# Sixteen batches of a fused convolution, attention and expert block: loops written out, value tiles spread, the residual added by identity products, the next input loaded by channel halves

## What is computed

```python
# 1. convolution attention over channels (32 inner channels)
q, k, v = conv1x1(x, Wq, bq), conv1x1(x, Wk, bk), conv1x1(x, Wv, bv)
x = conv1x1(softmax(q @ k) @ v, Wo, bo) * gamma + x
# 2. differential attention over the tokens, 8 heads of width 32
t = tokens(x); n = layer_norm(t)
a = softmax(q1 @ k1.T / s) - lam * softmax(q2 @ k2.T / s)       # q1, k1, q2, k2, v from n
t = t + group_norm(a @ v) @ out_w.T + out_b
# 3. shared expert and 8 routed experts (the best 2 are kept), hidden width 128
n = layer_norm(t)
t = t + shared(n) + sum_e(combine[e] * expert_e(n))
```

## Time and profile before

| what | us |
|---|---|
| median of 3 runs | 6143.56 |
| lowest and highest run | 6142.13, 6154.33 |
| the profiled execution's own time | 6151.38 |
| span of its trace | 6149.6 |
| TensorE busy | 5867.3 (95% of the span) |
| VectorE busy | 4669.8 (76%) |
| ScalarE busy | 3217.5 (52%) |
| GpSimd busy | 3090.5 (50%) |
| mean granted clock of TensorE | 0.977 of full |

### The profile page before, as it was taken

How to read it: one execution, slowest core, us unless ns; L and a number is a source line. 1 busy time by engine, 2 the same in 40 slices (tenths; PEclk the granted TensorE clock), 3 DMA queues, 4 the chain that set the end, 5 groups by cost and what they waited for, 6 DMA issues and landing times.

```text
span 6149.6 us, 126831 instructions
## 1 busy us (share of the span) xinstructions
PE 5867.3 (95%) x41264; PEld 3809.3 (62%) x41264; DVE 4669.8 (76%) x6583; ACT 3217.5 (52%) x5788; POOL 3090.5 (50%) x1382
## 2 busy tenths in 40 slices
PE   6999999999999999999999999999999999999999
PEld 3566566655656556566665766657666566665666
DVE  5867778687786877868778787786877778677786
ACT  3645546455564545636456464554645546455464
POOL 2826638175380744807447083571825728256281
PEclk8999999999999999999999999999999999999999
DMA  2212222222222212222222221222212222121221
GB/s 75 58 46 61 58 53 54 60 51 58 51 50 60 55 56 52 48 60 57 56 51 48 62 58 54 53 50 60 59 48 55 49 61 59 46 58 47 65 58 46
DMA packets 148332, 338.95 MB, mean 55 GB/s; under 512 B 38224, under 2 KB 60880, under 8 KB 139216
## 3 DMA queue, kind: packets, MB, share of 16 engines
q1 hardware_dynamic: 146128, 329.32, 22.0%
q10 hardware_dynamic: 1536, 1.05, 0.1%
HBM read 90.49 MB, written 17.30 MB: 18 GB/s over the span
## 4 chain that ended last, share of the span: by engine, by line
PE 76%; DVE 9%; issue 7%; ACT 3%; DMA 2%; POOL 2%; DVEq 0%; ACTq 0%; SPq 0%; POOLq 0%
PE psum L1049 17%; PE psum L1265 16%; PE psum L1190 14%; PE psum L1211 13%; PE psum L1349 6%; DVE minus_max L773 6%; PE psum L1218 4%; PE psum L1309 2%; POOL prob_sums L379 2%; PE psum L1196 1%; PE psum L1098 1%; DMA prob_sums<-combine_rows_dram 1%; ACT probs L523 1%; DVE small L688 1%; PE psum L1111 0%
## 5 line engine op out<-in xcount | busy, mean ns | idle before, releaser
L379 POOL TENSOR_TENSOR prob_sums<-probs 128x1024 f32<-128x1024 f32 x752 | 1795.7, 2389 | 2892.2 <-ACT probs L523 2559.2
L523 ACT ACTIVATE probs<-psum 128x512 f32<-128x512 f32 x4096 | 2214.2, 595 | 1376.0 <-PE psum L1265 1341.1
L773 DVE TENSOR_REDUCE minus_max<-psum 128x1 f32<-128x1024 f32 x2048 | 2400.3, 1209 | 413.6 <-PE psum L1190 409.6
L1265 PE MATMUL psum<-stack 98*128 98x512 f32 x4096 | 1430.7, 434 | 2.5 <-DVE max_rows L783 1.8
L379 POOL TENSOR_TENSOR prob_sums<-prob_sums,probs 128x1024 f32<-128x1024 f32 x512 | 1219.3, 2381 | 44.4 <-ACT probs L523 6.6
L1190 PE MATMUL psum<-stack 96*128 96x512 f32 x4096 | 1198.8, 406 | 25.2 <-DVE minus_max L773 24.5
L1211 PE MATMUL psum<-probs,v_tokens 128*32 128x256 f32 x16384 | 1126.2, 389 | 5.8 <-ACT probs L523 5.8
L1265 PEld LDWEIGHTS psum<-stack 98*128 98x128 f32 x4096 | 702.5, 191 | 543.4 <-ACT probs L523 326.5
L1190 PEld LDWEIGHTS psum<-stack 96*128 96x128 f32 x4096 | 757.1, 192 | 258.8 <-DVE minus_max L773 68.0
L1211 PEld LDWEIGHTS psum<-probs,v_tokens 128*32 128x32 f32 x16384 | 423.4, 109 | 487.4 <-issue 271.0
L1049 PE MATMUL psum<-act_hi,w_hi 128*128 128x512 f32 x1730 | 690.5, 399 | 19.4 <-DVE act_lo L752 11.0
(11 more groups left out here) (153 smaller groups left out, 4680.3 us busy)
## 6 DMA issues: line engine op xcount, KB each, us to landing
stack<-stage SPq DMA_DIRECT2D x1024, 128.0 KB, 3.0
stack<-stage SPq DMA_DIRECT2D x256, 256.0 KB, 3.0
prob_sums<-combine_rows_dram SPq DMA_DIRECT2D x128, 256.0 KB, 3.8
stage<-combine_rows_dram SPq DMA_DIRECT2D x128, 256.0 KB, 4.3
x_tile<-x_dram SPq DMA_DIRECT2D x17, 1024.0 KB, 4.9
x_tile<-o_head SPq DMA_DIRECT2D x480, 32.0 KB, 1.9
stack<-max_rows SPq DMA_DIRECT2D x512, 4.0 KB
y_dram<-residual SPq DMA_DIRECT2D x16, 512.0 KB, 2.8
```

The source lines that it names most:

```text
L379: nc.gpsimd.tensor_tensor(total, first, probs[:, k % NP, :], ALU.add).then_inc(sum_pool, 1)
L523: nc.scalar.activation(probs[:, k % NP, half * HALF:(half + 1) * HALF], ps[:, exp_bank(k) + half, :], ACT.Exp).then_inc(p_ready, 1)
L773: v.tensor_reduce(nm[:, u % 2, q:q + 1], flat_in, AX.X, ALU.max, negate=True).then_inc(ring_free, 1)
L1265: mm(ps[:, exp_bank(k) + half, :], stack[0:KS, s, 1, kt * P:(kt + 1) * P], stack[0:KS, s, 0, half * HALF:(half + 1) * HALF], start=True, s ...
```

## The change

All loops over batches become straight code, on all five engines, so each wait compares with a constant. The value tiles stand behind the scores 0 to 3 and 5 to 7 of unit 0, and tile 7 behind the second score of unit 1. The residual goes into PSUM banks 0 to 3 by four plain float32 products with the identity, ahead of the output projection, which then accumulates onto it; what is left for the other engines is to add the bias and move the sum out, for channel tile 0 on ScalarE and for channel tile 1 on VectorE. `norm_groups(b, 1)` stands after the first high half of `project_out` and no longer after both. The next input is loaded by two transfers, one for each channel tile; the first waits only for `on_hi` of tile 0. `conv_vk` goes by channel tiles, with a wait for each.

```diff
-VALUES_BEHIND = {("score", 0, q): (q,) for q in range(6)}
-VALUES_BEHIND["turn", 0] = (6, 7)
+VALUES_BEHIND = {("score", 0, q): (tt,) for q, tt in ((0, 0), (1, 1), (2, 2), (3, 3), (5, 4), (6, 5), (7, 6))}
+VALUES_BEHIND["score", 1, 1] = (7,)
...
-                sp.wait_ge(on_lo, b * NH * CT + NH * CT)
-                sp.dma_start(xin[:, :, :], x[following].rearrange("(t p) n -> p t n", p=P)).then_inc(x_in, 16)
+                for t in range(CT):
+
+                    if t == 0:
+                        sp.wait_ge(on_hi, b * NH * CT + NH)
+                    else:
+                        sp.wait_ge(on_lo, b * NH * CT + NH * CT)
+                    sp.dma_start(xin[:, t, :], x[following].rearrange("(t p) n -> p t n", p=P)[:, t, :]).then_inc(x_in[t], 16)
...
-            with sp.Fori(0, B - 1) as b:
-                batch(b, b + 1)
-
-            batch(B - 1, B - 1)
+            for b in range(B):
+                batch(b, min(b + 1, B - 1))
...
-            with act.Fori(0, B) as b:
+            for b in range(B):
...
+                for half in range(NH):
+                    act.wait_ge(y1_full, b * 4 + 2 * half + 1)
+                    nc.scalar.activation(res[:, 0, half * HALF:(half + 1) * HALF], ps[:, 2 * half, :], ACT.Identity,
+                                         bias=vec(V_OUTB)).then_inc(y1_act, 1)
                 normalise(b)
...
-                for k in range(4):
-                    t, cols = k % 2, slice((k // 2) * HALF, (k // 2 + 1) * HALF)
-                    if k == 0:
-                        dve.wait_ge(res_in, b * CT + CT)
-                    dve.wait_ge(y1_full, b * 4 + k + 1)
-                    v.scalar_tensor_tensor(res[:, t, cols], ps[:, k, :], vec(V_OUTB + t), res[:, t, cols],
-                                           ALU.add, ALU.add).then_inc(y1_ready, 1)
+                for half in range(NH):
+                    cols = slice(half * HALF, (half + 1) * HALF)
+                    dve.wait_ge(y1_full, b * 4 + 2 * half + 2)
+                    v.tensor_scalar(res[:, 1, cols], ps[:, 2 * half + 1, :], vec(V_OUTB + 1), None, ALU.add).then_inc(y1_dve, 1)
...
-                        pe.wait_ge(y1_ready, n * 4 + tt // 2 + 2)
+                        pe.wait_ge(y1_act, n * 2 + tt // 4 + 1)
+                        pe.wait_ge(y1_dve, n * 2 + tt // 4 + 1)
...
-                for half in range(NH):
-                    project_out(0, half, False)
+                pe.wait_ge(res_in, b * CT + CT)
+                pe.wait_ge(g_var, b * CT + 1)
+                for k in range(4):
+                    mm(ps[:, k, :], ident(), res[:, k % 2, k // 2 * HALF:(k // 2 + 1) * HALF], start=True, stop=False)
+                project_out(0, 0, False)
                 norm_groups(b, 1)
+                project_out(0, 1, False)
...
-            attention(0)
-            with pe.Fori(0, B - 1) as b:
+            for b in range(B):
+                attention(b)
                 behind_attention(b)
-                attention(b + 1)
-            behind_attention(B - 1)
```

More of the change, by code:

```diff
@@ L211, in build @@
         filled = sem("constants_filled")
-        x_in, x_used, res_saved = sem("x_in"), sem("x_used"), sem("residual_saved")
+        x_in = [sem(f"x_in{t}") for t in range(CT)]
+        x_used, res_saved = sem("x_used"), sem("residual_saved")
         y_out = [sem(f"y_out{half}") for half in range(NH)]
@@ L232, in build @@
         on_ready, on_hi, on_lo = sem("on_ready"), sem("on_hi"), sem("on_lo")
-        y1_full, y1_ready = sem("y1_filled"), sem("y1_ready")
+        y1_full, y1_act, y1_dve = sem("y1_filled"), sem("y1_by_act"), sem("y1_by_dve")
         r_full, r_rows, r_z, r_exp, r_comb = sem("router_filled"), sem("router_rows"), sem("router_z"), sem("router_exp"), sem("combine_ready")
@@ L253, in _ @@
             sp.dma_start(raw_rest, w_split[:, W_DOWN:W_SPLIT]).then_inc(raw_in, 16)
-            sp.dma_start(xin[:, :, :], x[0].rearrange("(t p) n -> p t n", p=P)).then_inc(x_in, 16)
+            for t in range(CT):
+                sp.dma_start(xin[:, t, :], x[0].rearrange("(t p) n -> p t n", p=P)[:, t, :]).then_inc(x_in[t], 16)
             def load_keys(n):
@@ L356, in _ @@
             nc.gpsimd.memset(stack[AUX:P, :, :, :].bitcast(F32), 1.0).then_inc(filled, 1)
-            with pool.Fori(0, B) as b:
+            for b in range(B):
                 def add_head(h):
@@ L740, in _ @@
             assert taken[0] == FIRST_STEPS, taken[0]
-            with dve.Fori(0, B) as b:
+            for b in range(B):
                 taken[0] = 0
@@ L1067, in conv_q, with conv_vk @@
                 last.then_inc(q_full, 1)
-            def conv_vk(n, half):
-                if half == 0:
-                    pe.wait_ge(x_in, n * 16 + 16)
+            def conv_vk(n):
                 for kt in range(CT):
-                    last = mm(ps[0:3 * CR, 2 + half, :], wqvk[:, kt, :],
-                              xin[:, kt, half * HALF:(half + 1) * HALF], start=(kt == 0), stop=(kt == CT - 1))
-                last.then_inc(vk_full, 1)
+                    pe.wait_ge(x_in[kt], n * 16 + 16)
+                    for half in range(NH):
+                        last = mm(ps[0:3 * CR, 2 + half, :], wqvk[:, kt, :],
+                                  xin[:, kt, half * HALF:(half + 1) * HALF], start=(kt == 0), stop=(kt == CT - 1))
+                        if kt == CT - 1:
+                            last.then_inc(vk_full, 1)
             def conv_scores(n):
@@ L1129, in first_projection @@
                 return split_mm(wide(0)[:, half, :], W_QK, (C, P), slice(half * HALF, (half + 1) * HALF))
-            for half in range(NH):
-                conv_vk(0, half)
+            conv_vk(0)
             pe.wait_ge(vk_ready, NH)
@@ L1288, in layer_norm @@
                     tokens(b)
-                    for half in range(NH):
-                        pe.wait_ge(y1_ready, b * 4 + 4)
-                        conv_vk(b + 1, half)
+                    pe.wait_ge(y1_act, b * 2 + 2)
+                    pe.wait_ge(y1_dve, b * 2 + 2)
+                    conv_vk(b + 1)
                     for k in range(4):
@@ L1309, in project_out @@
                             last = mm(ps[:, k, :], wt[:, w:w + P], xx[:, kt, cols],
-                                      start=(kt == 0 and not low and n == 0), stop=(kt == CT - 1 and low))
+                                      start=False, stop=(kt == CT - 1 and low))
                         if kt == CT - 1 and low:
                             last.then_inc(y1_full, 1)
-                for half in range(NH):
-                    project_out(0, half, False)
+                pe.wait_ge(res_in, b * CT + CT)
[3 more added lines that the diff above has]
+                project_out(0, 0, False)
                 norm_groups(b, 1)
+                project_out(0, 1, False)
                 for half in range(NH):
```

## The result

| | median us | runs | ratio to before (95% interval) |
|---|---|---|---|
| before | 6148.16 | 4 | |
| changed | 6080.28 | 4 | 0.9889 (0.9872 to 0.9906) |

The changed kernel is 1.1% faster, some 68 us, where 1.9% were forecast; the time lies 4 us above the stated range. The direction was right; of the 115 us that were forecast some 47 are missing.

The account below looks back on a forecast made before the run. TensorE's own work bounds the kernel, three quarters of what the end waited for. Per batch -1.3 - 2.2 - 3.7 = -7.2 us, times 16 = -115 us, gives 6028 us against the median of 6143.56; range 5998 to 6076.

Parts of the forecast that it names:

- Loops written out: All engines: register instructions ahead of waits cost 0, bound 0 to 1 us per batch; TensorE's jump costs 1.1 us.
- the other two terms: Start of attention, -1.3 - 2.2 us per batch, and the stretch behind attention, -3.7 us per batch.
- The slower rival: Straight code starves an engine through instruction fetches; 0.30 us apiece on TensorE would eat the gain; chance 0.03.
- The jump: TensorE's loop branch behind attention: costs 1.1 us of waiting beyond the cover of ScalarE's normalised heads.
- Values spread: Start of attention: -1.3 us per batch of idle time, -2.2 us from the clock no longer halving in most batches.
- The thin place: Little TensorE work between value tiles 6 and 7; halves the clock briefly in one batch of three.
- Behind attention: End of attention to first transposition back: -3.7 us per batch against the mean of 20.7, ends -2.0 and -4.3.
- The halves: Next input behind attention: one whole load would make TensorE stand 2 us; halves make the gain real, add none.

Follow-up runs that it names:

- experiment 4: All five loops written out in the kernel before, nothing else: 6193.86 us, ratio 1.0076.
- experiment 3: ScalarE's loop alone written out in the kernel before: 6196.83 us, ratio 1.0079.
- experiment 1: Changed kernel with ScalarE's waits ahead of each Exp reordered, scores (`st_full`) first, then free buffers: 6036.82 us, ratio 0.9822 to before.
- experiment 7: The part behind attention alone in the kernel before, loops and value tiles as before: 6167.43 us, ratio 1.0027.
- experiment 6: The value tiles spread, alone, in the kernel before, all loops kept: 6091.08 us, ratio 0.9904.
- experiment 8: Changed kernel with both halves of the next input waiting for the last `on_lo`: 6078.46 us, ratio 0.9880 to before.

## Why the prediction was partly wrong

**Loops written out: the step that failed.** "I cost them at nothing", with a bound of 0 to 1 us of gain per batch. It was a cost, 49 us over the 16 batches from unit 1 on (3482.6 - 3433.9), shown by experiment 4, which has it alone. Put on top of 6028 it gives 6077, 3 us from the measured 6080.3. That it comes so close is in part luck: the other two terms gained some 8 us more than forecast, and against that stand 5 us by which the median before, now over 4 runs, lies above the one that the forecast was taken from, and some 3 us by which the rest of the span grew. Three things went wrong in that step. I asked only what the removed instructions cost, not what takes their place: the wait itself changed its instruction. I compared the first batch's attention (248.65) with the second's (247.44) and called it "not longer", when the 1.2 us was for the most part the very effect, on TensorE: from unit 1 on, at full clock in both, the first batch took 0.90 us more (215.41 against 214.51), and its units 1 to 3 took 41.93 us against 41.73:

```profile
121.26:163.19 41.93, 41.54 (x367) 1.00 0.28 62
```
And I wrote that the comparison is silent on the other engines, and bounded them on the side of gain alone. Experiment 3 shows that ScalarE's loop by itself brings 41 of the 49 us.

**The slower rival** had the right place and the wrong mechanism and price: not the fetch of instructions. It is excluded by experiment 1, whose straight code is as long as the changed kernel's and takes 42 of the 49 us back by the order of waits alone; experiment 3 has the same longer units while TensorE keeps its loop. The Trainium skill (Runtime: NRT & Kernel Launch, Instruction fetch mechanics) names the fetch at a taken branch as one reason why kernels prefer full unrolling. The jump's cost is real in these traces, 3.09 us of standing in experiment 7 and 1.1 us beyond the cover before. But full unrolling alone made this kernel 0.8% slower; the measurement decides.

**The jump.** Right: the first product now starts within 0.1 us of the end of attention, as this row shows beside the window's start at 713.97.

```profile
713.90 3.70 PE L1324 MATMUL psum<-residual,w_full 128*128 128x512 f32 x8
...
718.35 0.28 PE L1167 MATMUL psum<-small,w_full 128*128 128x4 f32 x2
...
724.38 2.16 PE L1159 MATMUL psum<-w_full,residual 128*128 128x128 f32 x16
726.38 3.60 PE L1080 MATMUL psum<-x_tile,w_full 128*96 128x512 f32 x8
730.71 1.97 PE L1305 MATMUL psum<-w_full,stage 128*128 128x128 f32 x16 [0.73 <-ACT stage L419]
```

**Values spread.** Right, and a little too small: -1.3 - 2.2 per batch were -56 us, measured -61 in the changed kernel and -65 alone (455.1 against 520.2, experiment 6). The -1.3 came as forecast; the clock gave 2.7 and not 2.2. (In three of the eleven batches that I read as halved for 10.2 us a further 3.4 us of half clock stood just before.) The thin place did not halve the clock in one batch of three; it did so in none.

**Behind attention.** Right: -3.7 per batch were -59 us, measured -62. The group product stands 4.4 us behind attention's end (4.6 forecast), the identity products take 3.70 us (3.67), the transposition back starts at 16.7 (16.9). What was not seen is that this part rests on the first: without the straight code it makes the kernel slower (experiment 7).

**The halves.** The early issue of the first half is not what makes the gain real: with both halves late nothing is lost (experiment 8). There the first products of the input start 3.6 us after the issue at 720.59, the products ahead of them fill 3.2 of these, and the 0.47 us of standing fits into the time that the transposition back waits for ScalarE anyway (0.73 us in the changed kernel). The claim itself, that one load of the whole would cost 2 us, was not tested. An estimate: at the 4.9 us of the earlier trace rows it would land at 725.5, 1.3 us behind the products' start at 724.23, some 20 us over the 16 batches.

## What to carry to other kernels

When loops are written out or waits become constants, look at which of several waits stays at the instruction, and write the one that comes last in time where it stays: here first for constants, last for register values. A sequencer's view by source line shows that such an instruction stands there, and the semaphore in its record shows which wait it holds; the busy rows show neither. A part that looks independent can lean on another: here the identity products paid where nothing stood ahead of them, and cost time behind a jump.

## What the runs showed that was not expected

The same three waits in two orders are worth 43 us in one form of the kernel and -83 us in the other, in some 2000 steps: 0.02 us and 0.04 us for each. The engine on which it happens is busy for half of the span only; what counts, as I read it, is that its latency lies between two steps of the engine that is full. And the clock at the start of attention fell in 15 of 16 batches although no idle stretch of TensorE there was longer than 1.62 us. It stayed up in all 16 once the same products were spread more evenly over a stretch 1.4 us shorter, in which the longest idle stretch was 0.80 us.
